# Moving the set-up work of a fused attention and routed-block kernel around its first scores

## What is computed

```
q, k, v = heads(x @ w_q.T), heads(x @ w_k.T), heads(x @ w_v.T)
q, k    = rms_norm(q), rms_norm(k)
scores  = tanh(q k^T / sqrt(8) / 50) * 50          # causal
x       = layernorm(x + softmax(scores) v @ w_o.T)
...
weights = x @ router_w + router_b                  # picks 63 tokens per batch
emb     = position * inverse frequencies           # cos(emb), sin(emb) rotate q and k
x       = layernorm(x + block(picked tokens) ...)
```

## Time and profile before

| | |
|---|---|
| median of 3 runs | 832.19 us (831.43 to 833.56) |
| profiled execution, its own time | 831.95 us |
| its span in the profile | 830.0 us |
| busy: PE, DVE, ACT, POOL | 82%, 72%, 67%, 47% of the span |
| first scores of batch 0 | 30.37 us from the span's start |
| first pv | 54.52 us |

### The profile page before, as it was taken

How to read it: one execution, slowest core, us unless ns; L and a number is a source line. 1 busy time by engine, 2 the same in 40 slices (tenths; PEclk the granted TensorE clock), 3 DMA queues, 4 the chain that set the end, 5 groups by cost and what they waited for, 6 DMA issues and landing times.

```text
span 830.0 us, 16995 instructions
## 1 busy us (share of the span) xinstructions
PE 678.9 (82%) x6576; PEld 401.4 (48%) x6576; DVE 595.4 (72%) x1681; ACT 554.2 (67%) x403; POOL 392.0 (47%) x399
## 2 busy tenths in 40 slices
PE   3588787889979988999899988998899879865652
PEld 2344334455546455645455545645565535434232
DVE  4442718777787788958888788769896986588455
ACT  0588688889768876959768876788687968600000
POOL 5263436447544574346455664446546543421201
PEclk8567678899789987989789987899799979985755
DMA  6321302033300503030304030120303030000001
GB/s 190 64 42 37 64 13 53 25 61 119 64 14 17 112 12 67 27 64 14 64 14 90 14 64 15 50 54 2 64 26 65 2 64 27 13 1 26 0 0 51
DMA packets 96913, 36.75 MB, mean 44 GB/s; under 512 B 68018, under 2 KB 94146, under 8 KB 96834
## 3 DMA queue, kind: packets, MB, share of 16 engines
q1 hardware_dynamic: 96834, 35.67, 18.8%
HBM read 14.69 MB, written 4.19 MB: 23 GB/s over the span
## 4 chain that ended last, share of the span: by engine, by line
PE 61%; DVE 18%; issue 10%; ACT 7%; POOL 3%; DMA 1%; POOLq 0%; DVEq 0%; ACTq 0%
PE ps_y L1199 16%; PE ps_s L1182 14%; ACT pr L731 4%; PE ps_m L1308 3%; PE ps_m L1230 3%; ACT th L716 3%; PE ps_m L1206 3%; PE ps_a L1230 3%; PE ps_m L1356 2%; PE ps_a L1393 2%; DVE v_aug L844 2%; PE ps_m L1258 2%; PE ps_a L1206 2%; PE ps_a L1258 1%; PE ps_a L1292 1%
## 5 line engine op out<-in xcount | busy, mean ns | idle before, releaser
L716 ACT ACTIVATE th<-ps_s 128x1024 f32<-128x1024 f32 (+1 forms) x256 | 280.2, 1129 | 110.7 <-PE ps_s L1182 102.0
L627 POOL TENSOR_TENSOR pr<-pr,tri 128x320 f32<-128x320 f32 (+1 forms) x256 | 194.8, 784 | 186.7 <-ACT pr L731 186.7
L731 ACT ACTIVATE pr<-th 128x2304 f32<-128x2304 f32 x128 | 271.5, 2122 | 15.5 <-PE ps_y L1199 15.4
L1182 PE MATMUL ps_s<-q_st,k_st 32*64 32x512 f16 (+7 forms) x2048 | 193.1, 319 | 24.9 <-ACT th L716 20.8
L1199 PE MATMUL ps_y<-pr,v_aug 128*32 128x512 f32 (+7 forms) x2048 | 157.4, 439 | 0.4 <-POOL pr L627 0.4
L1182 PEld LDWEIGHTS ps_s<-q_st,k_st 32*64 32x64 f16 x2048 | 92.3, 114 | 120.0 <-issue 54.3
L1199 PEld LDWEIGHTS ps_y<-pr,v_aug 128*32 128x32 f32 x2048 | 57.0, 113 | 66.9 <-issue 47.4
L641 POOL TENSOR_TENSOR st<-qk,st 128x1024 f16<-128x1024 f32 x32 | 73.8, 2327 | 32.3 <-DVE st L860 32.3
L629 POOL TENSOR_TENSOR k_wide<-qkT,head_of 128x1024 f32<-128x1024 f32 x16 | 30.1, 1902 | 58.0 <-DVE qkT L1029 58.0
L629 POOL TENSOR_TENSOR r<-x,rw_row 128x512 f32<-128x512 f32 x16 | 18.9, 1180 | 63.6 <-DVE x L922 63.6
L702 ACT ACTIVATE hq<-hu 128x512 f32<-128x512 f32 x8 | 5.0, 630 | 60.7 <-POOL hu L629 60.7
(11 more groups left out here) (220 smaller groups left out, 1133.9 us busy)
## 6 DMA issues: line engine op xcount, KB each, us to landing
x_in<-in_L_attn_x SPq DMA_DIRECT2D x16, 256.0 KB, 2.8
x_res<-in_L_attn_x SPq DMA_DIRECT2D x16, 256.0 KB, 3.1
result<-y_out SPq DMA_DIRECT2D x16, 256.0 KB, 2.4
mask_a<-in_L_ffn_attention_mask SPq DMA_DIRECT2D x3, 1024.0 KB, 5.2
pr<-in_L_ffn_attention_mask SPq DMA_DIRECT2D x2, 1024.0 KB, 8.6
w_sb<-in_L_ffn_w SPq DMA_DIRECT2D x2, 256.0 KB
q_st<-st SPq DMA_TRANSPOSE x16, 4.5
k_st<-st SPq DMA_TRANSPOSE x16, 4.7
```

What stands on the lines that cost most here:

```text
L627: return nc.gpsimd.tensor_tensor(buf, buf, tri[:, None, :].to_broadcast([P, blocks, 64]), ALU.mult)
L716: nc.scalar.activation(th[:, gi % 2, c0:c1], ps_s[:, c0:c1], ACT.Tanh, scale=1.0 / (QK_SCALE ** 2 * DH ** 0.5 * SOFTCAP))\
L731: nc.scalar.activation(pr[:, probs_at(n):probs_at(n) + GROUP], th[:, gi % 2, :], ACT.Exp, scale=SOFTCAP).then_inc(exp_done, 1)
L1182: last = mm(ps_s[64 * s:64 * s + 64, COL[kb]:COL[kb] + S - 64 * kb], k_st[rows, k, gi // 2, 64 * kb:64 * kb + 64], q_st[rows, k, gi // 2, ...
```

## The change

It has five parts, all in the set-up and in the preparation of batch 0.

1. The identity has a semaphore of its own (`ident_ready`) and is filled and selected ahead of POOL's other constants. PE's first transposes wait for it and the weights alone. PE no longer waits for DVE's copy `wT` before x's transposes; that wait stands ahead of the qk matmuls of batch 0. The other constants are waited for in `setup_routed`.
2. For batch 0, DVE makes the squares (in `prep_ss`) and both low parts (behind the casts in `prep_split`). POOL skips them.
3. For batch 0, the copies of v to `v_aug` stand behind the low parts. Their steps `va`, `vb` form a track `val` of their own, and `pv` waits for it.
4. On PE, `setup_routed` moves from behind `prep_v` to behind the second unit of the scores of group 0. DVE's part stays behind `prep_split`, now also behind the values' copies. Its end, the four slices of `trig`, becomes `setup_trig`, behind `prep_split` of batch 1.
5. On ACT, the sine moves from the stream's start to just ahead of the exp of group 1.

```diff
+            nc.gpsimd.memset(ident[:, :], 0.0).then_inc(ident_ready, 1)
+            pool.wait_ge(ident_ready, 1)
+            nc.gpsimd.affine_select(out=ident[:, :], in_=ident[:, :], compare_op=ALU.not_equal, fill=1.0, base=0,
+                                    pattern=[[-1, P]], channel_multiplier=1).then_inc(ident_ready, 1)
...
@@ scalar
-            act.wait_ge(setup_ve, SETUP_RED)
-            nc.scalar.activation(turn[:, :, :, :], red[:, :, :, :], ACT.Sin).then_inc(setup_act, 1)
...
+                        if n == 1:
+                            act.wait_ge(setup_ve, SETUP_RED)
+                            nc.scalar.activation(turn[:, :, :, :], red[:, :, :, :], ACT.Sin).then_inc(setup_act, 1)
                         nc.scalar.activation(pr[:, probs_at(n):probs_at(n) + GROUP], th[:, gi % 2, :], ACT.Exp,
@@ vector
-            v.wait_ge(const_ready, 19)
...
             def prep_ss(b, k):
+                if b.no == 0:
+                    ve["prep"].wait(v, b, "qk1")
+                    pl["prep"].done(nc.vector.tensor_tensor(qk2, qk_flat, qk_flat, ALU.mult), "sq", b)
...
                 if b.no == 0:
+                    ve["prep"].wait(v, b, "hi_k")
+                    for s, part in enumerate("qk"):
+                        pl["prep"].done(nc.vector.tensor_tensor(lo_parts[s], qk_twice[s], hi_parts[s], ALU.subtract),
+                                        f"lo_{part}", b)
+                    prep_v(b, k, True)
                     setup_routed()
+                if b.no == 1:
+                    setup_trig()
@@ tensor
-            t_.wait_ge(const_ready, 19)
+            t_.wait_ge(ident_ready, 2)
...
-            t_.wait_ge(setup_ve, 1)
...
+                    ve["val"].wait(t_, b, "vb")
...
                 ve["prep"].wait(t_, b, "xT")
+                if b.no == 0:
+                    t_.wait_ge(setup_ve, 1)
...
-                if b.no == 0:
-                    setup_routed()
...
                             scores(g[0], g[1], g[2], half)
+                        if g and g[0].no == 0 and g[2] == 0 and half == 1:
+                            setup_routed()
```

More of the change, by code:

```diff
@@ L75 @@
 VE_STEPS = {
-    "prep": ["xT", "qk0", "qk1", "va", "vb", "ss"] + rsqrt_of("qkr", 1, True) + rsqrt_of("qkr", 2) +
+    "prep": ["xT", "qk0", "qk1", "ss"] + rsqrt_of("qkr", 1, True) + rsqrt_of("qkr", 2) +
         ["qkn", "hi_q", "hi_k"],
+    "val": ["va", "vb"],
     "fin": ["yU0", "rd0", "y0", "yU1", "rd1", "y1", "yT", "res"] + moments_of(NT) + rsqrt_of("ln", 1) +
@@ L246 @@
     "fin.y1T/0": ["fin.y0/0@0", "route.rank/1@-1"],
-    "fin.y1T/1": ["prep.vb/1@1", "route.thr/1@-1"],
-    "fin.yT/0": ["late.x2@-2", "prep.vb/0@1"],
+    "fin.y1T/1": ["val.vb/1@1", "route.thr/1@-1"],
+    "fin.yT/0": ["late.x2@-2", "val.vb/0@1"],
     "fin.yT/1": ["fin.y1/1@0"],
@@ L251 @@
     "late.sc1": ["fin.yT/0@2", "late.x2@0"],
-    "late.w2": ["att.oT@0", "prep.vb/0@3", "route.thr/0@1"],
+    "late.w2": ["att.oT@0", "val.vb/0@3", "route.thr/0@1"],
     "prep.qk0/0": ["prep.xT/0@0"],
@@ L255 @@
     "prep.qk1/0": ["prep.qk0/1@-1", "route.rank/0@-2"],
-    "prep.qk1/1": ["fin.yT/0@-1", "prep.vb/0@0", "route.thr/1@-2"],
+    "prep.qk1/1": ["fin.yT/0@-1", "val.vb/0@0", "route.thr/1@-2"],
     "prep.v/0": ["prep.qk0/0@0", "route.thr/0@-2"],
     "prep.v/1": ["prep.qk1/1@0"],
-    "prep.xT/0": ["prep.vb/1@-1", "route.row/0@-2"],
+    "prep.xT/0": ["val.vb/1@-1", "route.row/0@-2"],
     "prep.xT/1": ["fin.res/0@-1", "prep.qk1/0@0", "sel.qkT@-2"],
@@ L469, in tracks @@
         def tracks(engine, steps):
-            return {n: Track([sem(f"{engine}_{n}{k}") for k in range(2 if n in ("prep", "fin", "route") else 1)], names)
+            return {n: Track([sem(f"{engine}_{n}{k}") for k in range(2 if n in ("prep", "val", "fin", "route") else 1)], names)
                     for n, names in steps.items()}
@@ L478, in at @@
             return {"a": ps_a, "m": ps_m}[BANK[use if unit is None else f"{use}/{unit.k}"]]
+        turned_weights = ps_m if BANK["prep.xT/0"] == "a" else ps_a
         block = ctx.enter_context(nc.Block())
@@ L835, in prep_qk, with prep_v @@
                     at(f"prep.qk{i}", b)[:, :].rearrange("p (n c) -> p n c", n=8)), f"qk{i}", b)
-            def prep_v(b, k):
+            def prep_v(b, k, last=False):
+                if b.no == 0 and not last:
+                    return
                 pe["prep"].wait(v, b, "v")
@@ L843, in prep_v @@
                     rows = slice(64 * s, 64 * s + 64)
-                    ve["prep"].done(nc.vector.tensor_copy(
+                    ve["val"].done(nc.vector.tensor_copy(
                         v_aug[rows, k].rearrange("p b n c -> p (b n) c")[:, :, 16 * s:16 * s + DH],
```

19 lines of the change are left out of this document (12 added, 7 removed).

## The result

The changed kernel took 845.18 us (median of 4 runs, 840.82 to 845.68), the kernel before 831.84 in the same series: a ratio of 1.0145 [1.0108, 1.0182], some 12 us slower by this ratio of the means and 13.3 by the medians. The forecast was 834.6 with a range up to 836.9. The direction was right; the size was not, and the time is outside the range. The profiled execution took 845.41, its span 843.7 us against 830.0.

A forecast was written before the change was run, and what follows sets the result against it. It took a serial chain to bound the kernel up to the first scores, then ACT, then PE from the first pv. Terms -2.09 + 1.07 + 1.05 + 0.15 + 2.90 - 0.42 = +2.66 on 831.95 gave 834.6, range 830.9 to 836.9.

The forecast's parts named there:

- x's transposes: On PE, they would begin at about 5.95 instead of 6.56 with the identity first: gain 0.6 us.
- reduce: On DVE, it would start at 13.8 instead of 15.19, with 0.77 us gained by the squares on DVE.
- first scores: On PE, they would start at 28.28 instead of 30.37, a gain of 2.09 us.
- tanh of group 2: On ACT, it would start at 39.0, after router set-up costs of 1.07 and 1.05 us.
- loads and sine: On ACT, two table loads around Sin, between tanh of group 2 and exp of group 1: cost 2.90 us.
- tanh of group 5: On ACT, it would start at 55.05 instead of 51.97, 3.08 us later.
- first pv: On PE, first product of probabilities and values: at 57.2 instead of 54.52, with 0.42 us regained from POOL's mask wait.
- Rival (c): PE's clock rises later than 57 us relative to pv, adding 1.2 to 1.5 us: 836.0; chance 0.12.
- (a): ACT's added work disappears in waits on PE after the first pv, leaving only gains: 829.4; chance 0.12.
- (b): PE's clock is up before group 2, shrinking set-up matmuls, transposes, scores and pv: 831.8; chance 0.10.
- (e): A drain on ACT leaves an idle gap of 1.4 us at each of two table loads: 837.4; chance 0.03.
- (d): Moved vector work costs on DVE what it costs on POOL, losing 0.77 + 1.3 of the gain: 836.6; chance 0.05.

The follow-up runs named there:

- the sine alone: Kernel before with only the sine moved ahead of the exp of group 1 and trig's copies behind prep_split of batch 1: 843.39 us, ratio 1.0131.
- the front: Kernel before with parts 1 to 3 of the change alone, router set-up and sine left where they were: 841.87 us, ratio 1.0116.

## Why the prediction was wrong

**Right, step by step, for 57 us.** x's transposes at 5.93 (forecast 5.95), reduce at 13.77 (13.8), q's issue at 21.34 (21.4), first scores 28.22 (28.28), tanh of group 2 at 38.93 (39.03), loads and sine 2.91 (2.90) with no drain between, tanh of group 5 at 54.89 (55.05), first pv at 56.96 (57.18) without POOL's wait. By the bare sum the first pv is 2.44 late; forecast was 2.66.

**Rival (c), part of it.** The clock rose later against pv, and the first 32 pv matmuls took 4.74 instead of 4.21, 0.53 more. Rivals (a), (b) and (e) are refuted: nothing was hidden by the first pv, the clock was 0.50 until 57, and the loads have no gaps (41.26 + 1.28 = 42.54, sine at 42.55). So is (d): the low parts took 1.18 each (2.36 for two), where I took 1.23.

**The step that failed** is the last sentence of the first part: "What is late at the first pv is late at the end, since nothing behind it waits for something that the delay leaves alone." Two things are left alone by a delay. The granted clock is one: its changes are no instruction, their place against the start is the execution's, and by group 22, at 148 us, the work has fallen in with them. The order of DVE and POOL at an operation that both start within a tenth of a microsecond is the other.

So the lateness at the first pv was not kept even before the steps. It was 2.44 there, and the shift 5.1 at group 10 and 3.4 at group 54, of which 0.1 is the clock's own place; with the sine alone, 3.0 us late at the first pv, nothing was left over. That 3.4 lies near the forecast of 2.66 is luck. Behind group 54 the clock rose one stretch later, two small operations of DVE ran under POOL's mask, PE stood 0.9 us longer, and the clock stayed down for some 20 us. This step and the later ones made the missing 10 us: over the whole span the mean granted clock was 0.817, against 0.828 before. A lateness of 3.4 us kept to the end would have given 835.4, inside the range. The execution that keeps to the old course with its wasted microsecond has a shift of 4.6 at group 126 and a span 7.2 longer than before, so its last 2.6 us arise in the tail.

**The range was too narrow for the same reason.** Its bounds came from the first 60 us alone. A delay of 3.3 us gave +7, one of 0.3 gave +17, and no kernel that moved work had a median below 834.3. The rival that was missing reads: any edit, whatever it moves, can put the work of 800 us on another course of the clock, and one instruction more on an engine is enough. Its price could not be had from the trace of before. What could be seen there is that PE is at the low clock for a good part of the span (mean 0.828), and that rows of DVE and POOL start at the same hundredth (482.74).

**What the kernel before is.** A repeat of it and two edits that move nothing (the unused semaphore and the last instruction) took 832.4 to 833.9. The changed kernel and fifteen others that moved work, or put an instruction ahead of it, took 834.3 to 849.6, with the front or without. It stands on a favourable course among them. Tuning by small steps and keeping what measures best would lead to such a kernel; that is an inference, no run shows it.

## What to carry to other kernels

When an edit is worth 1 us in 800, measure its shift as well as the time: put the starts of one regular instruction of both traces side by side. Do the same with the clock's changes, and take their displacement off the flat part; what is left over need not be the price of the edit either (here -3.4, 0, 3.4 or 6.8 for edits that moved the first pv by anything from -1.8 to +5.1). The price of a part is read close to it, where the clock is the same in both traces. The steps behind belong to the clock and to engines that collide. Further kernels with an idle microsecond ahead, or one instruction more, say how much of a loss belongs to the course: the changed kernel lost 13 us, and 5 with the idle microsecond. And the range of a forecast needs a term for that, which in this kernel was 0 to 17 us, and is added whatever the edit does.

## What I had not expected of the hardware

- One memset of 128x1 in DVE's first microsecond, where it waits anyway, made 832 us into 848.7, while an idle multiplication at the end made no difference (832.78).
- The work falls in with the granted clock's changes: traces of the same instructions that stand 0.7 us apart at group 1 stand 1.8 apart at group 54, as the clock's changes do.
- The order in which DVE and POOL start is worth 0.62 us on a 128x1024 multiply: 1.23 with both starting at 482.74, 1.85 when POOL was 0.09 ahead.
- A DVE operation over 8 columns took 0.72 us under POOL's mask instead of 0.17.
- The steps behind group 54 cost the changed kernel some 10 us of 845, 1.2%, at four or five places far behind its start, with 24 us more at the low clock. The Trainium skill (TensorE: Matmul & The Clock Gate, Part 1) puts the clock's penalty at a kernel's start below 1% of a typical span and says that it varies from run to run. Here the whole span varied less between runs of one program (66 of 69 runs of the kernel before took 830.5 to 836.7, the others 839.0 to 843.9; 848.01 to 849.15 with the idle memset first) than between programs.
- An idle delay can pay: 1 us of it took the changed kernel from 845.2 to 838.5, and the front alone from 841.9 to 834.3.
